# Edge attention on one core: ScalarE's step of the sort in another order

## What is computed

```python
qkv = x @ qkv_w + qkv_b                       # q, k: 4 heads x 8; v: 4 heads x 16
s, t = edge_index
qe = q[s] * scale + (edge_attr @ q_rpe_w + q_rpe_b)
ke = k[t] + (edge_attr @ k_rpe_w + k_rpe_b)
ve = v[t] + (edge_attr @ v_rpe_w + v_rpe_b)
compat = einsum('ehd,ehd->eh', qe, ke)
ex = exp(compat - segment_max(compat, s)[s])
attn = ex / (segment_sum(ex, s)[s] + 1e-16)
out = segment_sum(ve * attn, s)
return layernorm(x + out)
```

## Time and profile before

| | us |
|---|---|
| median of 3 runs | 6712.76 |
| lowest and highest | 6689.97, 6715.67 |
| the profiled execution, device time | 6723.71 |
| the profiled execution, span of the profile | 6722.0 |
| mean granted TensorE clock of it | 0.701 of full speed |
| HBM traffic | 122 GB/s over the span |

### The profile page before, as it was taken

One profiled execution on the slowest core, in us unless ns is written; L12 is line 12 of the kernel. 1 busy time (PEld: TensorE's weight loads), 2 busy tenths in 40 slices (PEclk: granted clock), 3 DMA queues, 4 the chain that ended last, 5 costly groups with the idle time before them and its releaser, 6 DMA issues. The chain is left out here.

```text
span 6722.0 us, 113212 instructions
## 1 busy us (share of the span) xinstructions
PE 3642.7 (54%) x22344; PEld 3336.9 (50%) x22344; DVE 4669.1 (69%) x18275; ACT 3058.9 (46%) x7584; POOL 3596.2 (53%) x4030
## 2 busy tenths in 40 slices
PE   4654555545545555554555555545455554386786
PEld 3544445444445444444445454445454444365665
DVE  7986666666666666666666666666666666598998
ACT  5964444444444444444444444444444444322332
POOL 0025555555555555555555555555555555565664
PEclk8976665666666666666666666666666666698999
DMA  2013333333333333333333333333333333497897
GB/s 74 19 48 93 95 94 95 98 95 96 97 96 95 97 96 95 94 97 95 98 96 96 94 96 97 93 95 98 92 96 95 96 96 94 133 374 305 339 367 269
DMA packets 628039, 821.65 MB, mean 122 GB/s; under 512 B 216092, under 2 KB 561885, under 8 KB 615007
## 3 DMA queue, kind: packets, MB, share of 16 engines
q1 hardware_dynamic: 510185, 373.02, 21.9%
q0 software_dynamic: 117824, 448.32, 18.1%
HBM read 644.87 MB, written 176.01 MB: 122 GB/s over the span
## 5 line engine op out<-in xcount | busy, mean ns | idle before, releaser
L542 POOL DMA_INDIRECT rec_dram<-recs,place_i x3232 | 3093.7, 957 | 2751.9 <-DVE recs L596 1828.1
L630 PE MATMUL ps_cnt<-hi_hot,lo_hot 128*128 128x98 bf16 x3232 | 371.1, 259 | 2563.8 <-ACT free_rec L691 1615.5
L674 ACT ACTIVATE lo_hotT<-lo_b,minus_p 128x512 f32<-128x512 bf16 x808 | 582.9, 721 | 2585.8 <-DMA w_in<-kv_dram 2300.2
L573 DVE SCALAR_TENSOR_TENSOR matches<-src_b,src_f,ps_const 128x128 bf16<-128x128 int16 (+3 forms) x3232 | 1582.3, 543 | 67.7 <-issue 52.5
L630 PEld LDWEIGHTS ps_cnt<-hi_hot,lo_hot 128*128 128x128 bf16 x3232 | 239.0, 120 | 2730.4 <-issue 2420.5
L639 PE MATMUL ps_look<-free_rec,lo_hotT 128*128 128x98 f32 x6464 | 1408.2, 389 | 2.9 <-ACT lo_hotT L680 2.9
L656 PE MATMUL ps_feat<-w_in,edge_in 115*128 115x128 f32 x6464 | 1348.3, 375 | 44.8 <-issue 44.5
L582 DVE CUSTOM_DVE_ANT_0 picked<-hi_hot,ps_look 128x98 f32<-128x98 bf16 x3232 | 642.3, 252 | 1015.2 <-remote 803.0
L639 PEld LDWEIGHTS ps_look<-free_rec,lo_hotT 128*128 128x128 f32 x6464 | 1286.1, 294 | 3.1 <-ACT lo_hotT L680 3.1
L656 PEld LDWEIGHTS ps_feat<-w_in,edge_in 115*128 115x128 f32 x6464 | 1247.9, 286 | 43.6 <-issue 43.4
L962 PE MATMUL ps_sum<-msg,ident 128*128 128x256 f32 x2744 | 624.5, 386 | 237.7 <-DVE msg L1176 237.7
(11 more groups left out here) (152 smaller groups left out, 3419.1 us busy)
## 6 DMA issues: line engine op xcount, KB each, us to landing
lo_b<-lo_dram SPq DMA_DIRECT2D x808, 128.0 KB
src_b<-src_dram SPq DMA_DIRECT2D x808, 128.0 KB
dst_b<-dl_dram SPq DMA_DIRECT2D x808, 96.0 KB
rec_dram<-recs,place_i POOLq DMA_INDIRECT x3232
edge_in<-in_attr SPq DMA_DIRECT2D x808, 36.0 KB
w_in<-kv_dram SPq DMA_DIRECT2D x808, 36.0 KB
kv_dram<-kvt SPq DMA_DIRECT2D x14, 336.0 KB, 2.7
xt<-in_xT SPq DMA_DIRECT2D x14, 224.0 KB, 3.3
```

The costliest lines, as they stand in the source:

```text
L542: pool.indirect_dma_start(rec_dram[:, :], bass.IndirectOffsetOnAxis(place_i[j][:, m:m + 1], 0), recs[j][:, m, :], None).then_inc(scattered ...
L573: last = dve.scalar_tensor_tensor(matches[j][:, m, 0:before], src_b[j][:, 0:before], src_f[:, bass.ds(u * CT + m, 1)], ps_const[:, CT - m: ...
L630: last = nc.tensor.matmul(ps_cnt[:, 0:NB], lo_hot[j][:, m, :], hi_hot[j][:, m, :], start=False, stop=False, skip_group_check=True)
L674: act.activation(lo_hotT[j][:, :], lo_b[j][:, :], ACT.Abs, bias=minus_p[:, 0:1]).then_inc(lo_off, 1)
```

## The change

In each step ACT now does records(u-1) first, then the table copy of u, and then offsets(u+2) and turned(u+2), one right behind the other. Before it began with offsets(u+2), and the records stood last. No instruction is added or taken away and no wait is dropped; nothing changes on the other engines but line numbers, which are one lower behind the edit (the table copy's own line is L692, where it was L691).

```diff
             def step(u, j, turn):
                 ahead, ahead_turn = slot(j, turn, -2)
-                if not ends(u, 2):
-                    offsets(u + 2, ahead, ahead_turn)
+                if not starts(u, 1):
+                    before, before_turn = slot(j, turn, 1)
+                    records(u - 1, before, before_turn)
                 act.wait_ge(counted, u + 1)
                 act.activation(free_rec[(j + 1) % 2][:, :], ps_cnt[:, 0:NB], ACT.Copy).then_inc(table_ready, 1)
                 if not ends(u, 2):
+                    offsets(u + 2, ahead, ahead_turn)
                     turned(u + 2, ahead)
-                if not starts(u, 1):
-                    before, before_turn = slot(j, turn, 1)
-                    records(u - 1, before, before_turn)
```

## The result

The changed kernel takes 6516.69 us (median of 4 runs, 6502.32 to 6526.29) against 6711.2 us for the kernel before in the same comparison. The ratio is 0.9714, 95% interval 0.9686 to 0.9743: 2.9% or 195 us faster. The forecast was 90 us, the right way but less than half of what came. The profiled execution took 6521.84 us.

What follows compares the result with a forecast made beforehand. SP's issuing of loads around POOL's sends was taken to bound the sort. Removing 90 us of SP's waits for PE from the median 6712.8 us gave 6623, rounded to 6620 us; range 6400 to 6800, forecast alone 6560 to 6680.

Steps and rivals of the forecast that it cites:

- SP's issue bounds the sort, and POOL's sends slow it: Sort: SP's issuing of loads around POOL's sends sets the pace, 6.68 us a unit; ACT, PE and DVE have slack.
- the example of 12.89 us: Sort, 3017.52 to 3030.41: one unit's loads took 12.89 us while POOL sent without a break, against 3.94 with POOL idle.
- rivals A: Sort: SP's pace is all that counts, so no change, 6680 to 6745 us; chance 28%.
- Rival C: Sort: sends close up and SP starves, 8.95 us per unit changing sides; 6860 us at 16 units; chance 20%.
- The copy's place makes the gain, through SP's waits for PE: Sort: an earlier copy lets PE start sooner, removing most of SP's waits for PE's features, 90 of 110 us.
- If it is cut, DVE stays closer behind the loads and little else happens, as long as SP is as slow as now.: Sort: DVE's wait before pick, 915 us, was not counted as gain, since SP would set the time again.
- Rival B: Sort: DVE's wait before pick goes, giving back a third to a half of 915 us, 6250 to 6400 us; chance 12%.
- The trap of the scatters ahead of the copy: ACT's step: if POOL's scatters of u-5 were late, copy, count, look and offsets would queue behind records; charged nothing.
- my charge of nothing for the records' new place: ACT's step: records ahead delay the copy 0.470 us, only where ACT doesn't wait anyway; their waits were charged nothing.
- PE's wait for the copy falls below 500 us: Sign in the changed profile: PE's wait for the table copy falls from 1355 us to below 500.
- SP's waits below 30 us, ACT's wait for loads near 1900, POOL's idle time for dots near 1100.: Signs in the changed profile: SP's waits fall from 94 us to below 30; ACT's and POOL's stay about as before.
- The rule that a DMA's start is small beside the DMA: Skill rule against the forecast: SP wouldn't set the pace, and the 915 us before pick could return, about 5800 us.

Runs made afterwards that it cites:

- copy first: Only the table copy moved ahead of offsets, records left last, against the kernel before: 5397.3 to 5399.21 us on unslowed occasions, 6466.70 us on a slowed one.

## Why the prediction was wrong

- *SP's issue bounds the sort, and POOL's sends slow it.* Right in the main for these occasions: moving one DMA of five off SP gave 128 us. But SP isn't slow wherever POOL sends; it is slow mainly from 3 us into a stretch on. And the example of 12.89 us held a wait: SP's last load started at 3026.82, and then SP waited until 3029.73 for PE's features, 2.9 us of the 81.4 in the earlier trace rows. The 12.89 us that priced rivals A and C (8.95 us for each unit that changes sides) thus took a wait for issuing, and one long example for the rule: from the first to the last load of a unit it is 4.85 us on the mean of that window, not 9.30. The forecast didn't know either that there are occasions without the slowing.
- *The copy's place makes the gain, through SP's waits for PE.* Right, and a little larger than I took it: 94 us in 4500 became 1.4 in 4300. The 46 waits that the earlier trace rows calls remote were for PE's features too, by the semaphore that ended them. I had counted four fifths of 110 us; it is 111 us, (94.2/674 - 1.4/666) x 808.
- *"If it is cut, DVE stays closer behind the loads and little else happens, as long as SP is as slow as now."* This is the step that failed. DVE's wait before pick was cut from 763/674 = 1.13 to 269/666 = 0.40 us a unit, DVE did close up, and SP was not as slow as before: of the 197 us in the sort some 86 remain when SP's waits are taken off. They are in SP's own pace, which I had held constant: without its waits a unit took SP 6.54 us before and takes 6.45 now. Why its pace rose is open. Rival B named DVE's wait; of its two signs one came (269 us, below 500), the other didn't (6.46 us a unit, not under 6.4), and 6517 us lies between its range and that of the forecast.
- *The trap of the scatters ahead of the copy.* It didn't spring. ACT waits there 20.2 us for PE by name, and 242.5 us in 83 waits that the view calls remote; the semaphore that ended each of the 83 is that of PE's features, 4.9 us on the mean after their modelled end. But my charge of nothing for the records' new place doesn't hold up: with the copy alone moved the gain is 255 us, so the place cost some 60. Whether it did so by these waits isn't shown.
- *PE's wait for the copy falls below 500 us.* Wrong, 1143 us. I overlooked that the copy, though ahead of the wait for unit u+2, stands behind the same wait of the step before. It gains one unit's loads of lead and no more.
- *SP's waits below 30 us, ACT's wait for loads near 1900, POOL's idle time for dots near 1100.* The first holds; the others are 1536 and 913 us in 4300.
- Rival C, by which sends that close up would starve SP, wasn't seen: stretches became a little shorter, 1.54 and 1.46 units after 1.68.
- I read the Trainium skill's rule that the gain lies at the busiest engine ("Perfetto Trace Analysis", section "Identifying Performance Opportunities") as no change, 6713 us. That was my reading and not the page's: the same section says to find that engine's gaps and to make what it waits for come sooner. DVE is the busiest here, and its wait before pick fell from 1.13 to 0.40 us a unit; the 195 us don't speak against the rule. The rule that a DMA's start is small beside the DMA ("DMA: Bandwidth & Descriptors", section "Issuing engines are not separate DMA queues") fits the unslowed occasions, where SP idles; on the slowed ones moving one of SP's five DMAs in each unit gave 128 us.

## What to carry to other kernels

On an in-order engine put what another engine is waiting for ahead of a wait for a late load, and try the pieces one by one: the one that came along here cost some 60 of 255 us. A wait of 1.7 us at 2% of the bottleneck's time isn't the ceiling of a gain if the bottleneck's pace depends on what the others do meanwhile; then give a range that reaches past it. And measure the kernel before on several occasions first, as the order of the work was worth 2.9 to 3.9% on some and, for the copy alone, nothing on others.

## What the hardware showed

The same kernel took 6711 to 6728 us on some occasions and 5400 us on others, with single runs from 6675 to 6758 us and from 5397 to 5403 us, and none between. What differs is how fast instructions are issued beside POOL's sends. A unit's loads on an unslowed occasion (copy first), first and last, with sends starting every 1.26 us throughout:

```profile
2000.13 0.33 SPq L519 DMA_DIRECT2D edge_in<-in_attr  x1
...
2002.94 0.33 SPq L526 DMA_DIRECT2D w_in<-kv_dram  x1
```

```profile
2000.02 0.95 POOL L542 DMA_INDIRECT rec_dram<-recs,place_i  x1 [0.30 <-issue]
2001.27 0.96 POOL L542 DMA_INDIRECT rec_dram<-recs,place_i  x1 [0.30 <-DVE recs L596]
```

From the first to the last load it is 2.81 us here, and 9.30 us in the slowed kernel before beside the same kind of sends. From one load's start to the next it is 0.48 us on the mean here, though POOL never stops; on the slowed occasion it was 0.44 with POOL idle and 1.87 late in a stretch. Waits on an engine's own result are longer, too: DVE's last piece of dots loses 486 us in 4300 on a slowed occasion, and the waits of the unslowed run hold no such line at all. A slowed trace also lacks events: of DVE's 808 signals `ranked` it holds 466 in the kernel before and 429 in the changed one, an unslowed trace all of them. So part of the waits there stands under "issue", and the totals by name are lower bounds.

What sets an occasion apart, a chip, a neighbour or a setting, no run here shows. The record gives each comparison's chip a number: slowed were 15, 11, 9 and 1, unslowed 7, 14, 11, 11, 12 and 12 (the first comparison has none). Number 11 was unslowed, slowed and unslowed again within eight minutes, so the number alone doesn't decide it; whether it was the same chip each time isn't on record. With the slowing gone the bound is POOL, 4 sends of 1.26 us for a unit of 5.05 us.
